# First attention of a two-layer macaron block: probabilities transposed by DMA, the next queries' rotation moved, one row table for both layers

## The reference, cut to what matters

```python
    q = (x @ Wq.T).reshape(b, s, H, DH)
    k = (x @ Wk.T).reshape(b, s, KVH, DH)
    v = (x @ Wv.T).reshape(b, s, KVH, DH)
    q = q * cos + _rotate_half(q) * sin
    k = k * cos + _rotate_half(k) * sin
    ...
    scores = jnp.einsum('bhqd,bhkd->bhqk', q, k) * scale
    scores = jnp.where(mask[None, None, :, :], scores, -inf)   # iq >= ik - 128
    attn = jax.nn.softmax(scores, axis=-1)
    out = jnp.einsum('bhqk,bhkd->bhqd', attn, v)
    return out.transpose(0, 2, 1, 3).reshape(b, s, H * DH) @ Wo.T
```

## Time and profile before

| | us |
|---|---|
| three runs | 840.57, 841.95, 836.37 (median 840.57) |
| the profiled execution | 835.15 |
| its span | 833.3 |
| busy: PE, DVE, ACT, POOL | 712.8, 627.9, 458.0, 402.5 |

### The profile page before, as it was taken

One profiled execution on the slowest core, in us unless ns is written; L12 is line 12 of the kernel. 1 busy time (PEld: TensorE's weight loads), 2 busy tenths in 40 slices (PEclk: granted clock), 3 DMA queues, 4 the chain that ended last, 5 costly groups with the idle time before them and its releaser, 6 DMA issues. The chain is left out here.

```text
span 833.3 us, 17601 instructions
## 1 busy us (share of the span) xinstructions
PE 712.8 (86%) x5515; PEld 481.6 (58%) x5515; DVE 627.9 (75%) x1436; ACT 458.0 (55%) x1033; POOL 402.5 (48%) x412
## 2 busy tenths in 40 slices
PE   7898969999969999989898699765698498978985
PEld 3555447777637777655555466433586397645652
DVE  5989878778787878699977677544897687676656
ACT  3444568878758888545423266325474476324551
POOL 4544766667667667358636177324004320331440
PEclk9999979999999999999999799966799598998998
DMA  9999995000000000030001233300000010012324
GB/s 375 327 300 185 226 231 2 0 0 0 2 0 1 0 0 0 6 116 1 1 14 58 77 114 110 129 1 1 1 1 2 7 46 2 1 52 84 116 84 164
DMA packets 64945, 59.07 MB, mean 71 GB/s; under 512 B 29106, under 2 KB 59186, under 8 KB 64370
## 3 DMA queue, kind: packets, MB, share of 16 engines
q1 hardware_dynamic: 60706, 47.85, 23.7%
q0 software_dynamic: 3744, 10.26, 3.5%
q10 hardware_dynamic: 432, 0.15, 0.1%
HBM read 27.92 MB, written 30.33 MB: 70 GB/s over the span
## 5 line engine op out<-in xcount | busy, mean ns | idle before, releaser
L1492 PE MATMUL PS<-XT,WA 128*128 128x512 f16 x432 | 100.4, 380 | 0.0
L607 POOL TENSOR_TENSOR ARENA<-ARENA,ST 128x512 f32<-128x512 f32 x64 | 66.6, 1040 | 64.0 <-DVE ST L1278 64.0
L724 ACT ACTIVATE ARENA<-T 128x512 f16<-128x512 f32 (+1 forms) x56 | 35.2, 628 | 109.9 <-DVE T L1156 102.4
L1492 PE MATMUL PS<-WA,ARENA 128*128 128x256 f16 (+2 forms) x960 | 68.6, 212 | 12.9 <-DVE ARENA L1165 11.9
L1492 PEld LDWEIGHTS PS<-WA,ARENA 128*128 128x128 f16 x960 | 56.6, 97 | 29.4 <-DVE ARENA L1165 18.0
L566 POOL DMA_INDIRECT yt_rows<-WA,DIX x46 | 45.4, 987 | 55.4 <-ACT WA L856 43.4
L1492 PEld LDWEIGHTS PS<-XT,WA 128*128 128x128 f16 (+1 forms) x432 | 42.3, 98 | 44.1 <-issue 0.8
L1492 PE MATMUL PS<-KVR,ARENA 128*128 (+1 forms) x384 | 57.9, 279 | 7.9 <-DVE ARENA L1250 4.6
L1258 DVE TENSOR_REDUCE ST<-PS 128x2 f32<-128x512 f32 x64 | 43.9, 686 | 26.1 <-PE PS L1492 25.3
L757 ACT ACTIVATE ARENA<-PS,ST 128x256 f32<-128x256 f32 x128 | 59.3, 470 | 7.0 <-DVE ST L1261 6.8
L1492 PE MATMUL PS<-XT,WC 128*128 128x512 f16 x264 | 60.6, 379 | 2.4 <-DVE T L1149 1.4
(11 more groups left out here) (184 smaller groups left out, 1803.0 us busy)
## 6 DMA issues: line engine op xcount, KB each, us to landing
xs_rows<-ROUT SPq DMA_DIRECT2D x2, 9252.0 KB, 46.1
WA<-xs_rows SPq DMA_DIRECT2D x46, 129.0 KB
WB<-wb_dram SPq DMA_DIRECT2D x1, 4096.0 KB, 21.4
WC<-wc_dram SPq DMA_DIRECT2D x1, 2304.0 KB, 26.5
WA<-wa_dram SPq DMA_DIRECT2D x4, 512.0 KB, 6.8
WA<-wa_dram SPq DMA_DIRECT2D x1, 2048.0 KB, 12.7
WA<-yt_rows SPq DMA_DIRECT2D x4, 512.0 KB, 4.1
WB<-yt_rows SPq DMA_DIRECT2D x4, 512.0 KB, 5.8
```

Source lines behind the costliest of these rows:

```text
L607: pl.tensor_tensor(pr, pr, rs.broadcast_to([P, 2, S]), ALU.mult).then_inc(norm_done, 1)
L724: sc.activation(HH[r, a, 0, :], T3[r, :], ACT.Copy).then_inc(hid_hi, 1)
L1492: ins = te.matmul(dst, left(a), right(b), start=first and n == 0, stop=last and n == 2, skip_group_check=True)
```

## The change

1. PR0 gets four buffers. ACT and DVE now split the normalised probabilities themselves, from SBUF, into the float16 tiles PH0 (four buffers), two steps behind. SP then transposes both parts of an item with one DMA (128 partitions x 1024 float16, 256 KB) into PT0 (four buffers). PE no longer transposes; its product with the values is four steps behind instead of three, and the projection five instead of four. The attention output has two banks (6 and 7).
2. The next heads' queries have a second bank. PE computes them right behind the scores instead of last in the step. ACT swaps their halves first in the odd steps, before the exponentials; POOL's sine product goes before its normalisation; DVE's cosine product goes from the middle of the even steps to the end of the odd ones.
3. One table `xs_rows` serves both layers. SP fills it once at the beginning, and writes its last column anew behind the first layer's gathers.
4. p = 1 is written out as well on PE and ACT; the lagged steps at the ends of the halves get one step more.

```diff
-        PR0 = ARENA[:, 0:1024].rearrange("p (a n) -> p a n", a=2)
-        PT0 = ARENA[:, 1024:2048].bitcast(F16).rearrange("p (a s n) -> p a s n", a=2, s=2)
+        PR0 = [x[:, o:o + 2 * S] for x, o in ((ARENA, 0), (ARENA, 512), (ROUT, 512), (ROUT, 1024))]
+        PH0, PT0 = ([x[:, o:o + 2 * S].bitcast(F16).rearrange("p (s n) -> p s n", s=2) for x, o in homes]
+                    for homes in (((WA, A_N * JF), (WA, A_N * JF + 512), (WB, B_N * JF), (WB, B_N * JF + 512)),
+                                  ((ARENA, 1024), (ARENA, 1536), (WC, 0), (WE, 0))))
-        QB, OB = 4, 7
+        QB, OB = 4, 6
+        def query_bank(hf, a):
+            return odd_bank(hf) + 1 if a else QB
...
 (SP)
-            for table in XS:
-                t3 = table.rearrange("(a p) d -> p a d", p=P)
-                sp.dma_start(t3[:, :, 0:D + 1], ROUT[:, 0:D + 1]...).then_inc(dma_z, 16)
+            rows3 = XS.rearrange("(a p) d -> p a d", p=P)
+            sp.dma_start(rows3[:, :, 0:D + 1], ROUT[:, 0:D + 1]...).then_inc(dma_z, 16)
+            def free_rows():
+                sp.dma_start(rows3[:, :, D + 1:ROW], FREE[:, :]...).then_inc(dma_z, 16)
+            free_rows()
+            def probabilities(hf, p, x):
+                it = NS0 * hf + 4 * p + x
+                sp.wait_ge(ph_lo, it + 1)
+                after(sp, pv_done, it - 3)
+                sp.dma_start(PT0[x].rearrange("p s (g n) -> p (s g) n", n=P), PH0[x].rearrange("p s n -> p (s n)"),
+                             transpose=True).then_inc(pt_in[x], 16)
+            (for every half, p and x)
...
             expert_blocks(0)
+            free_rows()
             expert_blocks(1)
...
 (POOL, step0)
+                if x % 2 and more:
+                    rope_sine(r + 2 + x // 2, x // 2)
                 pool.wait_ge(recip_done, st + 1)
                 pl.tensor_tensor(pr, pr, rs.broadcast_to([P, 2, S]), ALU.mult).then_inc(norm_done, 1)
-                if x % 2 and more:
-                    rope_sine(r + 2 + x // 2, x // 2)
 (ACT, step0)
+                if x % 2 and more:
+                    rope_swapped(r + 2 + x // 2, query_bank(hf, x // 2), x // 2)
+                if item := lagged(p, x, 2, P0):
+                    act.wait_ge(norm_done, st - 1)
+                    after(act, pt_in[xx], turned_count(hf, pp - 1))
+                    sc.activation(PH0[xx][:, 0, :], PR0[xx], ACT.Copy, scale=SP).then_inc(ph_hi, 1)
                 (the two exponentials of st)
-                if lagged(p, x, 3, P0): ... OT0 high
-                if x % 2 and more: rope_swapped(...)
+                if lagged(p, x, 4, P0): ... OT0 high
 (DVE, step0)
-                if x == 0 and before:
-                    rope_cosine(r + 1, QB, 1)
-                if x == 2 and more:
-                    rope_cosine(r + 2, QB, 0)
-                if lagged(p, x, 2, P0):
-                    v.scalar_tensor_tensor(PT0[:, x % 2, 1, :], PS[:, bank, :], SP, PT0[:, x % 2, 0, :], ...)
+                if item := lagged(p, x, 2, P0):
+                    v.scalar_tensor_tensor(PH0[item[1]][:, 1, :], PR0[item[1]], SP, PH0[item[1]][:, 0, :], ...)
                 (the reciprocal of st; the low part of OT0, now lagged by 4)
+                if x % 2 and more:
+                    rope_cosine(r + 2 + x // 2, query_bank(hf, x // 2), x // 2)
 (PE, step0: behind the scores)
-                if lagged(p, x, 2, P0): ... four te.transpose of PR0 with IDF
+                if x in (0, 2) ... : queries(hf, 2 * p + 2 + x // 2, query_bank(hf, x // 2), ..., r + 1 + x // 2)
+                if item := lagged(p, x, 4, P0):
+                    pe.wait_ge(pt_in[xx], turned_count(hf, pp))
+                    after(pe, ot_lo, st - 5)
                     (product with the values, into bank OB + a)
+                if item := lagged(p, x, 5, P0): (projection)
-                if x in (0, 2) ... : queries(hf, ..., QB, ..., r + 2 + x // 2)
```

More of the change, by code:

```diff
@@ L189, in macaron @@
         YG = [w[:, 6928:8976].rearrange("p (u t k n) -> p u t k n", u=UPH, t=2, k=2) for w in (WA, WB)]
[L190 removed]
+        XS = nc.dram_tensor("xs_rows", [ROWS, ROW], F32, kind="Internal").ap()
         YT = nc.dram_tensor("yt_rows", [2 * ROWS + 2 * TOK, D], F32, kind="Internal").ap()
@@ L803, in attention0 @@
                     step0(hf, 0, x)
-                with act.Fori(1, P0 - 1) as p:
+                for x in range(4):
+                    step0(hf, 1, x)
+                with act.Fori(2, P0 - 1) as p:
                     for x in range(4):
@@ L948, in _ @@
             attention0(1, 2, 0)
-            for x in range(3):
+            for x in range(4):
                 step0(1, P0, x)
@@ L1270, in step0 @@
                     rope_low(r + 2, 0, QT0[:, 0, 1, :], QT0[:, 0, 0, :])
[L1271 to L1275, removed]
+                if item := lagged(p, x, 2, P0):
+                    dve.wait_ge(ph_hi, st - 1)
+                    v.scalar_tensor_tensor(PH0[item[1]][:, 1, :], PR0[item[1]], SP, PH0[item[1]][:, 0, :], ALU.mult,
+                                           ALU.subtract).then_inc(ph_lo, 1)
                 if lagged(p, x, 0, P0):
@@ L1688, in step0 @@
                     ins.then_inc(scores, 1)
[L1689 to L1698, removed]
+                if x in ((1, 2) if isinstance(p, int) and p == 0 else (0, 2)) and not (isinstance(p, int) and p >= P0 - 1):
+                    queries(hf, 2 * p + 2 + x // 2, query_bank(hf, x // 2), r + 2 + x // 2, r + 1 + x // 2)
+                if item := lagged(p, x, 4, P0):
                     pp, xx = item
                     g = pp // (GRP // 2)
-                    pe.wait_ge(pt_lo, st - 2)
-                    after(pe, ot_lo, st - 3)
+                    pe.wait_ge(pt_in[xx], turned_count(hf, pp))
+                    after(pe, ot_lo, st - 5)
+                    pt = PT0[xx].rearrange("p s (q k n) -> p s k q n", q=2, k=2)
                     for kt in range(2):
-                        ins = product(PS[:, OB, 0:S], lambda s: V0[:, s, TPH * hf + 2 * (xx % 2) + kt, ds(g * P, P)],
-                                      lambda s: PT0[:, xx % 2, s, kt * S:(kt + 1) * S], kt == 0, kt == 1)
+                        ins = product(PS[:, OB + a, 0:S].rearrange("p (q n) -> p q n", q=2),
+                                      lambda s: V0[:, s, TPH * hf + 2 * (xx % 2) + kt, ds(g * P, P)],
+                                      lambda s: pt[:, s, kt], kt == 0, kt == 1)
                     ins.then_inc(pv_done, 1)
-                if item := lagged(p, x, 4, P0):
+                if item := lagged(p, x, 5, P0):
                     pp, xx = item
-                    pe.wait_ge(ot_lo, st - 3)
+                    pe.wait_ge(ot_lo, st - 4)
                     for t in range(2):
@@ L1758, in attention0 @@
                     step0(hf, 0, x)
-                with pe.Fori(1, P0 - 1) as p:
+                for x in range(4):
+                    step0(hf, 1, x)
+                with pe.Fori(2, P0 - 1) as p:
                     for x in range(4):
```

57 lines of the change are left out of this document (30 added, 27 removed).

## The result

| | before | after |
|---|---|---|
| median of the runs, us | 839.45 (836.37 to 841.95) | 859.92 (855.88 to 860.81) |
| ratio, 95% interval | | 1.0236 [1.0187, 1.0286] |
| the profiled execution, its span | 835.15, 833.3 | 859.32, 857.5 |

A forecast was written before the change was run, and what follows sets the result against it. PE was taken to bound the loop before; a closed DVE-ACT chain with port collisions then makes pairs 7.55 us for 6.65, +25 us, plus 4 at the halves' ends: +29 from 838, 867 us (853 to 881, chance 0.52; range 838 to 925).

The forecast's parts named there:

- PE's relief: First attention's loop: transposes leave PE, its need per pair falls from 6.56 to 5.66 us; 28 us back if PE stayed bound.
- The closed chain and the port: Pair of steps: gapless DVE-ACT chain of 6.69 us by order alone, 7.55 with waits for POOL at the shared SBUF port.
- both collisions: Even scaling falls into POOL's add, +0.55 us; odd probabilities' low part waits for the sine product, delaying the reciprocal, +0.31.
- The term of 25 us: Both halves of the first attention: +0.90 us per pair over 28 pairs, seven of eight in each half.
- The transposing DMA: SP's queue: 3.2 us of SP per item, under a step's 3.78; landing 5.8 us against 6.2 of slack, barely hidden.
- rival (c): DMA queue bounds from 3.78 us of SP per item on; 921 us at 4.5, near 1960 at worst; chance 0.22.
- PE doesn't wait for a DMA: Sign in the loop: PE waits for the queries' low part or for exponentials, not for a DMA; no size given.
- The ends of the halves: Last product's wait for the DMA landing plus one more lagged step: +2 us per half, +4 together, bounds 0 and 10.
- The row table: One table fill dropped, second column write behind the gathers: hidden, 0 us, at most 55 if the cover were gone.
- (a): Rival, loop: order without collisions, only the 6.69 us chain, 6.8 with hand-overs; +8, 846 us; chance 0.13.
- (b): Rival, loop: the gain comes through, PE's 5.66 us bounds, pair under 6.4; -24, 814 us; chance 0.13.
- named signs: Loop: pair 7.5 us, PE's share near 0.75, scaling 0.7 even and 0.17 odd, low part 0.7 and about 1.2.

## Why the prediction was right, and where it was off

**PE's relief.** Right that it is used up. But the prediction let PE alone bound the loop before, and took 28 us as what PE could give. The rotation's chain stood at 6.56 us before and at 6.68 with the DMA and the old order; those 28 us were not to be had in either order without further edits.

**The closed chain and the port.** The period after, link by link, from the rows of the pair above, beside the prediction's terms:

| link | forecast | measured |
|---|---|---|
| odd reciprocal to even maxima | 1.18 | 1.00 |
| maxima to scaling | 0.72 | 0.71 |
| scaling to exponentials, with the collision | 0.20 + 0.55 | 0.85 |
| exponentials to output's high part | 0.92 | 0.91 |
| to the rotated head's high part, to the swap | 0.40 + 0.50 | 0.26 + 0.66 |
| swap to probabilities' high part | 1.23 | 1.23 |
| to the odd exponentials | 0.50 | 0.54 |
| to the odd reciprocal, with the collision | 1.04 + 0.31 | 1.26 |
| pair | 7.55 | 7.42 |

The mechanism is right and both collisions fall where they were laid. By the tile view and POOL's timeline all 32 even scalings fall into an instruction of POOL, 28 of them into the add. The collisions cost 0.64 (0.81 - 0.17) and about 0.22 (1.26 - 1.04), 0.86 together. That 0.86 was forecast too is luck in part: the terms were 0.55 and 0.31, off by 0.09 each way. That the order does it is shown by itself (7.31 with PE's transposes), that the scaling is on the chain by taking it away (6.57). How the loss splits between chain and collisions is read from rows only: no run has the new order without the collisions. The mis-sized term is the chain without collisions, 6.69, which comes to 7.42 - 0.86 = 6.56, by its first link (1.00 for 1.18): I had put the gap behind the cosine product from another step. By these rows the new order without collisions would stand where before stood, and the collisions make the loss.

The Trainium skill, "SBUF — State Buffer", SBUF: two separate sides, calls the shared pair "an exclusive lock, not a bandwidth split", for GpSimd that reads SBUF against a DVE instruction with two SBUF inputs or in a 2-port mode. The traces agree for the low part, which has two such inputs and ends 0.55 behind POOL. The scaling, a 128x2 instruction, has one SBUF input; whether it runs in a 2-port mode no run here tells. It ended 0.03 behind POOL all the same.

**The number of pairs.** I took 28. By the stages it is 19.6/0.75 = 26: the first and the last steps of a half aren't at the full period (the last normalisations are 2.6 us apart in both kernels, 215.16 behind 212.57 before, 225.24 behind 222.65 after). The term of 25 us came to 19.6: 0.15 us a pair too much made 4, two pairs too many the rest.

**The transposing DMA.** Hidden, as forecast, but by far more. The view of its line after:

```profile
L491 SPq DMA_TRANSPOSE ARENA<-WA x32: 1231/1232/1407, 120.6 to 364.3; - x32
L491 SPq DMA_TRANSPOSE WC<-WB x16: 1232/1232/1385, 127.7 to 366.6; - x16
L491 SPq DMA_TRANSPOSE WE<-WB x16: 1232/1232/1287, 132.1 to 367.9; - x16
...
DMA to landing us min/median/max: 3.0/3.1/4.5
```

1.23 us of SP where I took 3.2, 3.1 us to land where I took 5.8. My price per piece came from 4-byte pieces, and these transfers aren't paid like them; rival (c) was never near. The Trainium skill's 1309 ns for one 128x128 block ("VectorE: DVE Perf Modes", The three transpose paths) isn't added up over the eight blocks of one transfer: the whole lands in 3.1 us. The sign "PE doesn't wait for a DMA" was wrong: PE waits for these tiles 29 times, 18.5 us in all,

```profile
157.52 0.83 PE L1516 MATMUL PS<-ARENA,KVR 128*128 128x256 f16 x6 [0.45 <-DMA ARENA<-WA]
```

but it has run ahead, and that wait costs nothing, as the kernel without the DMA shows (7.45).

**The ends of the halves.** Forecast 2 us for each, together 4; the stages show 1.2 + 3.2 = 4.4, and most of this agreement is chance. From the last normalisation (364.98) to the last output copy of the second half (372.23) pass 7.25 us, 6.2 from its end, against 5.9: +0.3. At the first scatter of the second layer (664.53 before, 685.88 after) the distance from the last normalisation is 320.6 and 320.9. The other 2.8 us come behind the last scatter of results (813.13 and 834.55; 20.2 and 23.0 us to the end). The last product of the kernel, before and after:

```profile
824.38 1.48 PE L1492 MATMUL PS<-WC,ARENA 64*128 64x256 f16 x12 [2.85 <-DVE ARENA L1165]
```
```profile
847.44 2.60 PE L1516 MATMUL PS<-WC,ARENA 64*128 64x256 f16 x12 [2.76 <-DVE ARENA L1192]
```

The same twelve matmuls take 1.1 us more; the granted clock from 847 to 851 us is 0.58, near the lower level (1.2 GHz), and PE had waited for 2.8 us before them in both. The other 1.6 us lie between that scatter and this product (11.3 us before, 12.9 after): the granted clock behind the scatter is 1.00 before (813.13 to 816.00) and 0.50, the lower level, after (834.55 to 837.40), where PE is busy for the whole stretch in both. Of the thirteen profiles of this study five end 20.2 to 20.6 us behind that scatter and eight 22.9 to 23.2. All eight show 0.50 in the 1.5 us behind it and 2.6 to 2.7 us for the last product, the five show 1.00 and 1.48 us. The parts of the change lie on both sides: before with the new order and the changed kernel with the old one end early, before with one table ends late (2.62 us for that product) at the median of before. So these 2.8 us belong to the clock near the end and to no part of the change, and what puts it in the one or the other case stays open. Without them the two profiled spans differ by 21.4 us, close to the 20.5 of the medians. The lagged steps cost 1.2 + 0.3 = 1.5 us in place of 4; the landing alone was put 2.7 us too high at each end.

**The row table.** "0, it only frees the queue" holds for before (1.0002). The step left out that the price of not doing it had changed: with the DMA on the same queue it is 14 to 16 us, by which profile of the changed kernel one takes.

**Rivals.** (a) asked for no collisions: no even scaling of the changed kernel is without one. (b) asked for a pair under 6.4 us: 6.25 came only with the old order, no scaling and a moved copy. (c) asked for a DMA of 3.78 us of SP: 1.23. Of the named signs the pair, the scaling (0.81 and 0.17) and the low part (0.68 and 1.21) are as forecast; PE's share is 0.79 and not 0.75, since its busy time in a pair fell to 46.98/8 = 5.87 us and not to 5.66.

## What to carry to other kernels

Before relieving the busiest engine, follow one stage's operands around a whole period by distances of starts, over all engines: here two limits of equal length stood side by side, PE's work and the rotation's chain, and a longer chain was made by moving three instructions. Where several such chains are near each other, single edits hardly show (pairs of 6.65 and 6.61 us for 6.65) though both together take 0.40 us off a pair and make the kernel 1.2% faster than before. An instruction of 0.17 us that sits between a reduction and what everybody waits for can be worth folding into tables that exist already, since a neighbour's instruction of 1.3 us can fall on it; whether it pays depends on the chain (0.84 us a pair in the new order, nothing in the old one).

## What the runs showed of the hardware that I had not expected

- A DMA that transposes 128 partitions x 1024 float16 from SBUF to SBUF (256 KB, eight blocks) holds SP for 1.23 us and lands after 3.1 us, with 64 of them between 120 and 368 us and a DMA share of 0.37 from 154 to 214 us.
- A transposing DMA directly behind a write of 9216 single floats on SP's queue held SP for 18.9 us, though that write's own issue was over (31.2 us); one landed 21.3 us after its issue.
- The tiny scaling (128x2) takes mostly 0.74 to 0.93 us, and up to 1.25, in place of 0.17 where it falls into an instruction of POOL, and nearly always ends 0.01 to 0.04 us behind it; the low part, which reads two tiles of SBUF, ends 0.55 us behind, its own length nearly whole. POOL waits for DVE likewise: the add behind the low part takes 1.53 us for 1.26.
